# Expert tiles of a routed layer: plain f32 products against three products of high and low parts

## The chip, the core and the metric

One core of one Trainium2 chip runs the whole program. The metric is the device time of one launch in microseconds (us). Three runs of the kernel before gave 783.53, 786.41 and 776.94 us.

## The reference

2048 tokens of 256 numbers (`x`) pass four blocks, each added to `x` after a layer norm:

```
x = x + attn_a(norm(x))     # gated recurrence along the tokens, 6 heads of 64
x = x + ffn(norm(x))        # 8 experts, the best 2 per token
x = x + attn_b(norm(x))     # windowed attention, 16 heads of 16
x = x + ffn(norm(x))        # the same experts again

def ffn(h):
    probs = softmax(h @ router.T);  vals, idx = top_k(probs, 2);  vals /= vals.sum()
    for gup, dp, weight in experts:                  # gup 352x256, dp 256x176
        gate, up = split(h @ gup.T, 2)
        out += weight[:, None] * ((silu(gate) * up) @ dp.T)
```

All of it is float32.

## The kernel before

**Stages.** The program runs five stages, one after the other: the recurrence (0 to about 218 us of the profile), the expert tiles for the first time (222 to 334), the attention (lead-in 334 to 363, periods to 645), the expert tiles again (645 to 757), and the last adds and stores. Each stage's instructions stand in a `Block` (the one of `experts` is L1242); at its end all engines meet at a barrier, so the engine with the longest list holds the others.

**Routing.** Each token's row, with its weights and its number, is sent to the DRAM tensor `xs` by `pool_scatter` (L1181), an indirect DMA that GpSimd (POOL) issues: 8 per group of 512 tokens. Three of the four groups are sent before the expert stage. The last one is routed inside it: `pe_logits`, then compare and choose on VectorE (DVE), `pe_ranks`, and the 8 sends, which POOL issues in turn with its other work at tiles 3 to 10 (`SEND_AT`). The 39 tiles of 128 rows come in two parts (`PART`): tiles 0 to 16 need only the first three groups, tiles 17 to 38 need every row sent.

**One expert tile** (`experts`, L1188). SyncE (SP) loads 128 rows into `xin`, a ring of four (`load`, L1244 to L1257); before tile j+4 is loaded, tile j must have been turned and `aim` (L1417 to L1432, three small DVE operations that read `xin`) must be done. PE turns the rows (`x_transposed`, L1318), ACT copies them out (`x_out`, L1384), PE makes gate and up (`gate_up`, L1334, two products of 128x128 by 352 columns), ACT applies silu (L1391), DVE multiplies (`hidden`, L1439), PE turns the result (L1344), DVE copies it out (`hidden_out`, L1446), PE makes the second product (`down`, L1356, two of 88x128 by 256 columns), ACT scales it (`y_copy`, L1399) and POOL sends it to `back` (`send_back`, L1292). All operands are plain f32, and each such product stands in the trace as two records. PE's order in step s is gate_up(s), hid_transposed(s-1), x_transposed(s+1), down(s-2). SP also loads the attention's small weights in step 12 (`LEAD_FROM`).

**Products of split operands.** The recurrence and the attention use another way: an operand is split into a high part (ACT copies it into an F32R tensor) and a low part (DVE subtracts the high part), and a product is made as high by high, high by low and low by high, all F32R (L351, L362, L1701, L2229).

**Around the attention.** POOL fills the padding rows of `QS` and `KS` with 12 memsets (`pad`, L1829). They are issued within the first expert stage, between its sends. In the lead-in (`lead_*`, L1945 to L2000) SP brings the experts' results back, the four engines add and normalize pairs of blocks, and SP stacks the first keys and queries. The periods follow (`PERIODS`, 20 of them with 5 steps each; the program order of each engine is written out by step). Both expert weights of the second time are loaded by SP in period 15.

Of the kernel before, what the change touches and what calls it, by code (L numbers as in the profile page):

```python
# [62 lines left out]
def build(nc, t, out):  # L63

    ctx = ExitStack()
    with ctx:
# [14 lines left out]
        xTh = sb("xTh", [P, KD, PAD + T], F32R)  # L81
        xTl = sb("xTl", [P, KD, PAD + T], F32R)
# [92 lines left out]
        m = Routed(nc, ctx, t, sem, xTf)  # L175
# [8 lines left out]
        m.down.close()  # L184
        lead, periods = attention(nc, t, m, *common, ident)
# [11 lines left out]
def recurrence(nc, t, x, xn, xTh, xTl, xTf, yT, psY, bank, t0, tl, credit, tail_stats_dve, tail_xn_dve, tail_split_dve,  # L197
# [4 lines left out]
    with ctx:  # L202
# [33 lines left out]
        rms = sb("rms", [P, TPC * HA])  # L236

# [73 lines left out]
        with nc.Block() as block:  # L311
# [195 lines left out]
            def _(act):  # L507
# [49 lines left out]
                tail_act(act, t0, 0)  # L557
                def angle_weights(u):
                    act.wait_ge(folded, 7 + u)
                    act.activation(wfh[:, :, :, u * P:(u + 1) * P], kq[:, :, :, u * P:(u + 1) * P], ACT.Copy).then_inc(wfh_done, 1)  # L560
# [15 lines left out]
                for it in range(NCH):  # L576
                    squares(it)
                    means(it)
                    if it + 1 < NCH:
                        rounded(it + 1)  # L580
                    if it == 0:
                        tail_act(act, t0, 3)
                    else:
                        if it == 2:
                            act.wait_ge(m.filled, 16 * FILLS)
                        tail_rows_act(act, tl, it - 1)
                    if it + 1 < NCH:
# [12 lines left out]
            def _(pool):  # L600
# [34 lines left out]
                for it in range(NCH):  # L635
# [5 lines left out]
                    if it + 1 < NCH:  # L641
                        decays(it + 1)
                    if it > 1:
# [12 lines left out]
            def _(dve):  # L656
# [151 lines left out]
                for it in range(NCH):  # L808
# [27 lines left out]
                    if it > 0:  # L836
# [3 lines left out]
                        group.payload(xn)  # L840
                    if ahead:
# [9 lines left out]
                table.rows()  # L851


class Routed:


    def __init__(self, nc, octx, t, sem, xTf):
# [42 lines left out]
        self.sent, self.d_in = sem("f_sent"), sem("f_d_in")  # L900

    def open_down(self, nc, turn):
        self.wd = self.down.enter_context(nc.sbuf_tensor(f"f_wd{turn}", [FK, 2, NE * 2 * FH], F32, side="right"))

# [13 lines left out]

    def load_up(self, sp):
        for k in range(KD):  # L920
            sp.dma_start(self.gu[:, k], self.wgu_in_dram[k * P:(k + 1) * P]).then_inc(self.w_in, 16)
# [31 lines left out]
YB = 4  # L953
# [234 lines left out]
def experts(nc, m, x, xn, xTh, xTl, xTf, stats, meanvar, vareps, rstd, minus_half, bank, osem, sems, ident, last, lead=None,  # L1188
# [4 lines left out]
    XB = 4  # L1193
    SEND_AT = 3
    LEAD_FROM = 12
# [10 lines left out]
    with ctx:  # L1206
        def sb(name, shape, dt=F32):
            return ctx.enter_context(nc.sbuf_tensor(f"f{turn + 1}_{name}", shape, dt))

        xin = sb("xin", [P, XB, XW])  # L1210
        xt = sb("xt", [P, 2, D])
        act_g = sb("act_g", [P, 2, FH])
        hid = sb("hid", [P, 2, FH])
        hT = sb("hT", [FK, 2, 2 * P])
        yout = sb("yout", [P, YB, D])
        second = sb("second", [P, AR])
        share = sb("share", [P, AR])
        target = sb("target", [P, AR], U32)
        back = sb("back", [P, NGRP, 2, TPC, D]) if last else None

        psG, psH, psY = bank[0], bank[1], bank[2]
        psX, psZ = bank[3][:, 0], bank[3][:, 1]

        x_in = [sem(f"x_in{i}") for i in range(XB)]
        tx_done, xt_done = sem("tx"), sem("xt")
# [1285 lines left out]
```

## Time and profile before

| | |
|---|---|
| median of 3 runs | 783.53 us |
| lowest and highest | 776.94, 786.41 us |
| profiled execution, first to last instruction (its span) | 780.9 us |
| mean granted TensorE clock | 0.848 |
| busy: PE, DVE, POOL, ACT | 83%, 60%, 44%, 38% |

The profile gives no other time of its own execution than its span; the median is 2.6 us above it. In a row of the timeline stand the start, the time from the first start to the last end of the merged instructions, engine, line, operation, what is written from what, and in brackets how long the engine was idle before and for whom it waited. PE is the matmul side of TensorE. Matmuls are pipelined, so what counts is the distance between starts.

### The profile page before, as it was taken

The page shows a single profiled execution, that of the slowest core. Times are in us where ns is not written, and L with a number is a line of the kernel's source. Part 1 is how long each engine was busy: PE and PEld are TensorE (multiplying, and loading weights), DVE is VectorE, ACT ScalarE, POOL GpSimd, SP SyncE. Part 2 cuts the span into 40 slices and gives each one's busy share as a digit, 9 for nine tenths or more (in the row PEclk, how much of TensorE's full clock was granted, in tenths as well). Part 3 has the DMA queues.
Part 4 walks back from the last instruction along what each step waited for, and adds up shares of the span by engine and source line. Part 5 has one row for each costly group of instructions (what it writes and reads, how often), then busy time and mean ns, then how long its engine had stood idle before and what let it go on. Part 6 is the DMA issues. An engine that isn't in the chain of part 4 may idle for free. (4 is left out here: it accounts for less than half of the span.)

```text
span 780.9 us, 14537 instructions
## 1 busy us (share of the span) xinstructions
PE 645.8 (83%) x4707; PEld 503.9 (65%) x4707; DVE 466.2 (60%) x1226; ACT 296.7 (38%) x567; POOL 342.0 (44%) x406
## 2 busy tenths in 40 slices
PE   0889999994569999924689999999899868999960
PEld 0668787773447677713578788878778645777740
DVE  6894859787626434463665767876852454644423
ACT  1363444351014444432344545545433322444430
POOL 4304051616413767743513434445545470653335
PEclk9989999895858999956669999999965555999995
DMA  8699400151122633275432340431307211443329
GB/s 268 214 351 350 149 1 8 37 116 44 43 65 85 195 104 97 85 233 88 81 56 30 83 81 12 76 89 50 80 16 201 100 58 44 134 140 97 102 74 315
DMA packets 68317, 86.92 MB, mean 111 GB/s; under 512 B 8909, under 2 KB 62802, under 8 KB 67380
## 3 DMA queue, kind: packets, MB, share of 16 engines
q1 hardware_dynamic: 61428, 67.80, 32.4%
q0 software_dynamic: 6816, 18.19, 6.5%
q8 instruction: 41, 0.67, 0.4%
q14 instruction: 32, 0.26, 0.1%
HBM read 35.13 MB, written 39.06 MB: 95 GB/s over the span
## 5 line engine op out<-in xcount | busy, mean ns | idle before, releaser
L1292 POOL DMA_INDIRECT back<-f_yout,f_target x78 | 76.7, 983 | 113.7 <-ACT f_yout L1399 103.0
L1334 PE MATMUL bank<-f_wgu,f_xt 128*128 x312 | 113.7, 489 | 3.4 <-ACT f_xt L1384 3.3
L1181 POOL DMA_INDIRECT xs<-xn,f_slots x64 | 65.0, 1016 | 56.7 <-ACT xn L1172 41.1
L1439 DVE TENSOR_TENSOR f_hid<-f_act_g,bank 128x176 f32<-128x176 f32 x78 | 26.3, 338 | 104.5 <-ACT f_act_g L1391 100.4
L2066 POOL TENSOR_SCALAR_AFFINE_SELECT b_prob<-b_prob 128x512 f32<-128x512 f32 x60 | 38.1, 635 | 112.7 <-ACT b_prob L2307 112.4
L2307 ACT ACTIVATE b_prob<-bank 128x1024 f32<-128x1024 f32 x60 | 61.4, 1023 | 55.8 <-PE bank L2146 55.5
L1356 PE MATMUL bank<-f_wd,f_hT 88*128 x312 | 81.4, 385 | 0.0
L1334 PEld LDWEIGHTS bank<-f_wgu,f_xt 128*128 128x128 f32 x312 | 59.1, 199 | 31.3 <-issue 9.9
L2376 DVE COPY_PREDICATED bank<-b_later,bank 128x512 f32<-128x512 int32 x60 | 41.6, 694 | 47.0 <-PE bank L2116 42.4
L1356 PEld LDWEIGHTS bank<-f_wd,f_hT 88*128 88x128 f32 x312 | 54.2, 193 | 4.8
L1399 ACT ACTIVATE f_yout<-bank,f_share 128x256 f32<-128x256 f32 x78 | 36.9, 473 | 39.9 <-PE bank L1356 38.9
L1391 ACT ACTIVATE f_act_g<-bank 128x176 f32<-128x176 f32 x78 | 24.7, 317 | 67.0 <-PE bank L1334 67.0
L2380 DVE TENSOR_REDUCE b_m<-bank 128x4 f32<-128x512 f32 x64 | 44.2, 691 | 8.1 <-PE bank L2107 6.0
L2187 PE MATMUL bank<-b_prob,b_V 128*17 128x128 f32 x992 | 45.6, 307 | 2.1 <-POOL b_prob L2068 2.0
L2146 PE MATMUL bank<-b_QS,b_KS 64*128 64x128 f32 x496 | 45.7, 298 | 0.8 <-ACT b_prob L2307 0.6
L2068 POOL TENSOR_SCALAR_AFFINE_SELECT b_prob<-b_prob 128x512 f32<-128x512 f32 x64 | 40.9, 638 | 11.4 <-ACT b_prob L2304 11.4
L2146 PEld LDWEIGHTS bank<-b_QS,b_KS 64*128 64x128 f32 x496 | 40.8, 215 | 3.4 <-ACT b_prob L2307 2.2
L1384 ACT ACTIVATE f_xt<-bank 128x256 f32<-128x256 f32 x78 | 29.9, 383 | 26.0 <-PE bank L1318 17.7
L2116 PE MATMUL bank<-b_KS,b_QS 48*128 48x256 f32 x208 | 32.6, 362 | 7.8 <-DVE b_m L2380 7.7
L351 PE MATMUL bank<-xTh,wfh 128*128 128x512 f32 x64 | 30.2, 472 | 8.4 <-DVE wfl L705 8.4
L1344 PEld LDWEIGHTS bank<-ident_sb,f_hid 128*88 128x88 f32 x156 | 19.3, 125 | 21.7 <-issue 13.8
L1318 PE MATMUL bank<-ident_sb,f_xin 128*128 128x128 f32 x156 | 32.0, 289 | 1.5 <-DMA f_xin<-xs 1.5
(313 smaller groups left out, 1519.4 us busy)
## 6 DMA issues: line engine op xcount, KB each, us to landing
xs<-xTf SPq DMA_DIRECT2D x8, 2176.0 KB, 19.3
f_xin<-xs SPq DMA_DIRECT2D x78, 136.0 KB, 2.1
f_wgu<-in_wgu SPq DMA_DIRECT2D x4, 1408.0 KB, 14.3
f_wgu<-back SPq DMA_DIRECT2D x16, 256.0 KB, 5.1
b_KS<-b_kh SPq DMA_DIRECT2D x32, 128.0 KB, 3.9
b_QS<-b_qh SPq DMA_DIRECT2D x32, 128.0 KB, 3.9
f_back<-back SPq DMA_DIRECT2D x8, 512.0 KB, 7.5
f_wd<-in_wd SPq DMA_DIRECT2D x4, 968.0 KB
```

The lines of the kernel that those rows point to most:

```text
L1181: pool.indirect_dma_start(m.xs, bass.IndirectOffsetOnAxis(m.slots[:, g, c, i:i + 1], 0), xn[:, g * TPC + i], None)\
L1292: pool.indirect_dma_start(m.back, bass.IndirectOffsetOnAxis(target[:, g % AR:g % AR + 1], 0), yout[:, g % YB], None, bounds_check=2 * 2 * ...
L1334: mm = pe.matmul(psG[:, g % 2, 0:2 * FH], xt[:, g % 2, k * P:(k + 1) * P], m.gu[:, k, bass.ds(e, 2 * FH)], start=k == 0, stop=k == KD - 1)
L1356: mm = pe.matmul(psY[:, g % 2, 0:D], hT[:, g % 2, k * P:(k + 1) * P], m.wd[:, k, bass.ds(e, D)], start=k == 0, stop=k == 1)
L1399: act.activation(yout[:, g % YB], psY[:, g % 2, 0:D], ACT.Copy, scale=share[:, g % AR:g % AR + 1])\
L2066: pool.affine_select(halves_of[:, :, 0], halves_of[:, :, 0], [[0, 4], [-1, P]], ALU.is_gt, 0.0, base=0, channel_multiplier=1)
L2068: pool.affine_select(halves_of[:, :, 1], halves_of[:, :, 1], [[0, 4], [1, P]], ALU.is_ge, 0.0, base=0, channel_multiplier=-1).then_inc(kep ...
L2146: mm = pe.matmul(own_t[:, half, i, w], KS[rows, 2 * u + i, ring(b - 1 + w)], QS[rows, 2 * u + i, ring(b)], start=True, stop=True)
L2187: mm = pe.matmul(psO[CG * j:CG * j + HV1, u * P:(u + 1) * P], V[:, (b - 1 + w) % RING, 4 * u + j], prob[:, quad(b, u) % 2, half, c:c + P], ...
L2307: ins = act.activation(dst, psT[:], ACT.Exp, scale=SCALE)
L2376: dve.copy_predicated(own_s[:, :, :, 1], later[:].unsqueeze(1).unsqueeze(1).broadcast_to([P, 2, 2, P]), own_s[:, :, :, 0]).then_inc(sel_do ...
L2380: dve.tensor_reduce(mo[:, :, 2 * u:2 * u + 2], own_s[:, :, :, 1], AX.X, ALU.max).then_inc(m_done, 1)
```

## The change

- In `experts` both products become three products of F32R operands. Tokens: `x_high` (ACT copy) and `x_low` (DVE subtraction) replace `x_out`; hidden: `hid_high` and `hid_low` replace `hidden_out`.
- Tokens are turned two tiles ahead, into two halves of `bank[3]`; `down` follows three steps behind gate_up (`DOWN_AFTER`). PE's order in step s is gate_up(s), x_transposed(s+2), down(s-3), hid_transposed(s-1).
- The weights are split beforehand: the low part is written over the raw weights, the high part goes to new tensors (`guh`; `wdh`; the first time `wd_high` lies over `xTh`/`xTl`). First time: ACT copies and POOL subtracts quarters of gate/up in turns 1 and 2 of the recurrence; ACT copies and DVE subtracts quarters of down in its last turn, the last two at DVE's end. Second time: eighths of gate/up in periods 15 to 17 and of down in periods 18 and 19, ACT and DVE.
- The tile buffers lie over `QS` and `KS`. So the 12 memsets leave the first expert stage: POOL waits for the last sends, makes 4 before its part of the lead-in and 8 after it.
- The gate/up weights of the second time are loaded in periods 5 and 7, the down weights in period 16.

```diff
 recurrence, act, turn it, behind means(it):
+                    if 0 < it < NCH - 1:
+                        up_high(2 * it - 2)
+                        up_high(2 * it - 1)
+                    if it == NCH - 1:
+                        down_high(0)
+                        down_high(1)
...
 recurrence, pool, behind decays(it + 1):
+                    if 0 < it < NCH - 1:
+                        for q in (2 * it - 2, 2 * it - 1):
+                            pool.wait_ge(m.up_high, q + 1)
+                            m.up_low_part(pool, 0, q)
...
 recurrence, dve, last turn behind payload, and at the end:
                 table.rows()
+                for q in (2, 3):
+                    dve.wait_ge(m.dn_high, q + 1)
+                    m.down_low_part(dve, 0, q)
...
+    def up_low_part(self, eng, turn, q):
+        part = self.eighth(q) if turn else self.quarter(q)
+        eng.tensor_tensor(self.gu[:, :, part].bitcast(F32R), self.gu[:, :, part], self.gu_high[turn][:, :, part].bitcast(F32),
+                          ALU.subtract).then_inc(self.up_low, 1)
...
 experts, gate_up:
-                    pe.wait_ge(xt_done, g + 1)
+                    pe.wait_ge(xtl_done, g + 1)
...
                     for k in range(KD):
-                        mm = pe.matmul(psG[:, g % 2, 0:2 * FH], xt[:, g % 2, k * P:(k + 1) * P], m.gu[:, k, bass.ds(e, 2 * FH)],
-                                       start=k == 0, stop=k == KD - 1)
+                        for xx, w in ((xth, guh), (xth, gul), (xtl, guh)):
+                            mm = pe.matmul(psG[:, g % 2, 0:2 * FH], xx[:, g % 2, k * P:(k + 1) * P], w[:, k, bass.ds(e, 2 * FH)],
+                                           start=n == 0, stop=n == 3 * KD - 1)
+                            n += 1
...
 experts, pe:
                 x_transposed(0)
+                x_transposed(1)
                 for s in range(STEPS):
                     if s < G:
                         gate_up(s)
                     if s == RANKS_AT:
-                        pe_ranks(pe, m, turn, g3, psZ[:, P:2 * P])
+                        pe_ranks(pe, m, turn, g3, ranks)
+                    if s + 2 < G:
+                        x_transposed(s + 2)
+                    if 0 <= s - DOWN_AFTER < G:
+                        down(s - DOWN_AFTER)
                     if 0 <= s - 1 < G:
                         hid_transposed(s - 1)
-                    if s + 1 < G:
-                        x_transposed(s + 1)
-                    if 0 <= s - 2 < G:
-                        down(s - 2)
...
 experts, dve:
+                x_low(0)
+                x_low(1)
                 group.compare()
                 group.choose()
                 for s in range(STEPS):
                     if s < G:
                         hidden(s)
-                    if 0 <= s - 1 < G:
-                        hidden_out(s - 1)
+                    if s + 2 < G:
+                        x_low(s + 2)
                     if s < G:
                         aim(s)
+                    if 0 <= s - 1 < G:
+                        hid_low(s - 1)
...
 experts, pool:
-                    if not last and j >= LEAD_FROM and j % 2 == 0 and (j - LEAD_FROM) // 2 < lead["pads"]:
-                        lead["pad"](pool, (j - LEAD_FROM) // 2)
...
+                    for r in range(YB):
+                        pool.wait_ge(y_out[r], 16 * uses(tile_no(turn, G), r, YB))
                     lead["pool"](pool)
...
         def lead_pool(pool):
-            padded(pool)
+            for i in range(4):
+                pad(pool, i)
+            padded(pool, 1)
...
             pair_deviation(pool, FIRST_PAIRS)
+            pool.wait_ge(u_off, FIRST_PAIRS + 1)
+            for i in range(4, 12):
+                pad(pool, i)
+            padded(pool, RING // 2)
...
 attention:
+        UP_LOADS = {5: 0, 7: 1}
+        UP_PARTS = [(15, 0), (15, 3), (16, 0), (16, 1), (17, 0), (17, 1), (17, 3), (17, 4)]
+        DOWN_PARTS = [(18, 0), (18, 1), (18, 2), (18, 3), (18, 4), (19, 0), (19, 3), (19, 4)]
```

## Rows read from the trace of the kernel before

**Rows 1.** The page: busy time of PE, its granted clock in 40 slices

```profile
PE 645.8 (83%) x4707; PEld 503.9 (65%) x4707; DVE 466.2 (60%) x1226; ACT 296.7 (38%) x567; POOL 342.0 (44%) x406
PEclk9989999895858999956669999999965555999995
```

**Rows 2.** Timeline, one tile of the first expert stage

```profile
301.71 1.35 PE L1334 MATMUL bank<-f_wgu,f_xt 128*128 x4
...
302.90 0.38 PE L1344 MATMUL bank<-ident_sb,f_hid 128*88 128x128 f32 x2
...
303.34 1.03 PE L1356 MATMUL bank<-f_wd,f_hT 88*128 x4
...
304.20 1.35 PE L1334 MATMUL bank<-f_wgu,f_xt 128*128 x4
...
304.41 0.15 DVE L1431 SCALAR_TENSOR_TENSOR f_target<-f_second,f_xin 128x1 uint32<-128x1 f32 x1
```

**Rows 3.** Timeline, F32R products of 256 columns, at full clock and at half

```profile
424.95 0.28 PE L2229 MATMUL bank<-b_boh,b_oTl 128*128 128x256 f32 x1
...
425.07 0.28 PE L2229 MATMUL bank<-b_bol,b_oTh 128*128 128x256 f32 x1
...
640.19 0.41 PE L2229 MATMUL bank<-b_bol,b_oTh 128*128 128x256 f32 x1
...
640.41 0.41 PE L2229 MATMUL bank<-b_boh,b_oTh 128*128 128x256 f32 x1
```

**Rows 4.** One line, L1257 (the loads of a tile's rows): from issue to landing

```profile
DMA to landing us min/median/max: 2.0/2.1/4.0
```

**Rows 5.** Timeline, second expert stage: POOL's sends, the load of tile 17, the last copy

```profile
650.31 0.95 PE L1334 MATMUL bank<-f_wgu,f_xt 128*128 x1 [0.56 <-ACT f_xt L1384]
...
672.08 0.97 POOL L1292 DMA_INDIRECT back<-f_yout,f_target  x1 [1.52 <-DVE f_tiles L1133]
673.36 0.96 POOL L1181 DMA_INDIRECT xs<-xn,f_slots  x1 [0.30 <-DVE f_second L1426]
...
691.32 0.97 POOL L1181 DMA_INDIRECT xs<-xn,f_slots  x1 [0.30 <-ACT f_yout L1399]
...
696.91 0.38 PE L1318 MATMUL bank<-ident_sb,f_xin 128*128 128x128 f32 x2
...
755.00 0.47 ACT L1399 ACTIVATE f_yout<-bank,f_share 128x256 f32<-128x256 f32 x1 [0.39 <-PE bank L1356]
```

**Rows 6.** Timeline, recurrence: subtractions and copies on GpSimd and VectorE

```profile
14.93 3.38 POOL L609 TENSOR_TENSOR f_wgu<-gate,w 128x512 f32<-128x512 f32 x2
17.22 2.17 DVE L700 TENSOR_TENSOR f_wgu<-f_wgu 128x1024 f32<-128x1024 f32 x1
...
21.65 1.22 DVE L700 TENSOR_TENSOR f_wgu<-f_wgu 128x1024 f32<-128x1024 f32 x1
...
113.74 1.28 POOL L619 TENSOR_TENSOR sgl<-sg,sgh 12x512 fp32r<-12x512 f32 x1 [4.46 <-ACT sgh L523]
...
184.63 1.76 DVE L768 TENSOR_TENSOR gate<-gate,o 128x1536 f32<-128x1536 f32 x1
```

**Rows 7.** Timeline, the end of the recurrence on VectorE and ScalarE

```profile
216.07 0.17 DVE L1160 SCALAR_TENSOR_TENSOR f_done<-f_done,f_tiles 128x8 f32<-128x8 f32 x1
216.99 1.02 ACT L171 ACTIVATE xTf<-bank 128x1024 f32<-128x1024 f32 x1 [12.91 <-PE bank L162]
```

**Rows 8.** One line, L1829 (the memsets); timeline of the lead-in's end

```profile
L1829 POOL MEMSET b_QS<- x6: 1796/1798/1800, 272.0 to 319.1; 32x2048 f32 x6
...
358.24 0.20 POOL L1894 TENSOR_TENSOR b_u_shift<-b_u_rstd,b_u_mv 128x2 f32<-128x2 f32 x1
...
366.92 0.59 PE L2100 MATMUL bank<-b_eye,b_maskT 128*128 128x128 bf16 x4 [10.17 <-DMA b_QS<-b_qh]
```

**Rows 9.** Timeline, the attention's last chain

```profile
637.23 0.24 DVE L2403 RECIPROCAL b_rinv<-bank 128x16 f32<-128x16 f32 x1
...
644.58 0.38 ACT L2337 ACTIVATE xTf<-bank 128x256 f32<-128x256 f32 x1 [4.69 <-PE bank L2247]
```

More of the change, by code:

```diff
@@ L236, in recurrence @@
         rms = sb("rms", [P, TPC * HA])
+        m.gu_high.append(sb("guh", [P, KD, NE * 2 * FH], F32R))
         F = 2 * P
@@ L557, in _, with up_high, down_high @@
                 tail_act(act, t0, 0)
+                def up_high(q):
+                    act.wait_ge(m.w_in, 16 * KD)
+                    act.activation(m.gu_high[0][:, :, m.quarter(q)], m.gu[:, :, m.quarter(q)], ACT.Copy).then_inc(m.up_high, 1)
+                def down_high(q):
+                    act.wait_ge(m.d_in, 32)
+                    act.wait_ge(vg_ready, now(NCH - 1, NVG, NVG))
+                    act.activation(m.wd_high[0][:, :, m.quarter(q)], m.wd[:, :, m.quarter(q)], ACT.Copy).then_inc(m.dn_high, 1)
                 def angle_weights(u):
@@ L840, in _ @@
                         group.payload(xn)
+                    if not ahead:
+                        for q in (0, 1):
+                            dve.wait_ge(m.dn_high, q + 1)
+                            m.down_low_part(dve, 0, q)
                     if ahead:
@@ L1208, in sb @@
             return ctx.enter_context(nc.sbuf_tensor(f"f{turn + 1}_{name}", shape, dt))
[L1210 to L1219, printed above, removed]
+        xin, xth, xtl, act_g, hid, hTh, hTl, yout, second, share, target = m.tile_buffers
+        guh, wdh = m.gu_high[turn], m.wd_high[turn]
+        gul, wdl = m.gu[:].bitcast(F32R), m.wd[:].bitcast(F32R)
+        back = m.both_halves[:, 0:NGRP * 2 * TPC * D].bitcast(F32).rearrange("p (g e b d) -> p g e b d", g=NGRP, e=2, b=TPC)
         psG, psH, psY = bank[0], bank[1], bank[2]
-        psX, psZ = bank[3][:, 0], bank[3][:, 1]
+        psX = bank[3]
+        logits, ranks = psY[:, 0, D:2 * D], psY[:, 1, D:2 * D]
         x_in = [sem(f"x_in{i}") for i in range(XB)]
-        tx_done, xt_done = sem("tx"), sem("xt")
+        tx_done, xth_done, xtl_done = sem("tx"), sem("xth"), sem("xtl")
         gu_done, silu_done, hid_done = sem("gu"), sem("silu"), sem("hid")
-        th_done, hT_done = sem("th"), sem("hT")
+        th_done, hTh_done, hTl_done = sem("th"), sem("hTh"), sem("hTl")
         dn_done, y_done = sem("dn"), sem("y")
@@ L1453, in _ @@
                 group, table = Routing(dve, m, turn, g3), Table(dve, m, turn, 1)
-                group.take(psZ)
+                group.take(logits)
+                x_low(0)
+                x_low(1)
                 group.compare()
@@ L1567, in attention @@
         later = sb("later", [P, P], I32)
+        vbuf = sb("V", [P, RAW])
+        with ExitStack() as tiles_too:
+            routing.take_tile_buffers(nc, tiles_too)
         QS = sb("QS", [P, SLOTS, RING * P], F32R)
```

150 lines of the change are left out of this document (111 added, 39 removed).

## The prediction

> **What bounds the kernel now.** I read the page first: PE is busy for 645.8 of 780.9 us, more than any other engine, and its granted clock falls to half in a few stretches only, most of them in the attention [rows 1]. A busy share is an average, so each stage was then read by its own timeline.
>
> The expert tiles are bound by PE. In the timeline of one tile gate_up starts at 301.71 and the next at 304.20, a period of 2.49 us, and PE's own work fills it: gate_up until the transposes start at 302.90 (1.19), the transposes up to `down` at 303.34 (0.44), `down` until the next gate_up (0.86) [rows 2]. 78 such periods are 194 us. Two things other than PE stand at the edge of this stage. The load of a tile takes 2.0 to 4.0 us, 2.1 as a rule, from issue to landing [rows 4]. And in tiles 3 to 10 POOL issues two indirect DMAs per tile, 1.28 us apart, so 2.56 per tile, a little more than PE's period: the fifteen issues between 672.08 and 691.32 are evenly 19.2/15 = 1.28 [rows 5]. Tile 17 may only be loaded once the last of them has landed, and its transpose runs at 696.91 [rows 5], 46.6 behind the first gate_up at 650.31, in step 16: 16 periods are 39.8, its place in the step is 1.4, and the first tiles with the ranks of the last group take the other 5.4. PE doesn't idle ahead of it, so both limits fall together there.
>
> The recurrence is bound by VectorE with POOL and ScalarE beside it, and ends with VectorE's list at 216.24 and ScalarE's at 218.01 [rows 7]. The lead-in is a chain of small steps that ends in SP's stacking of the first keys; POOL's part is over at 358.44, and PE's first product runs at 366.92, waiting for that DMA [rows 8]. The attention's tail is a chain over VectorE, PE and ScalarE that ends at 644.96 [rows 9].
>
> **Tile period.** Six F32R products replace four records each time. F32R products of 256 columns follow each other in 0.12 us at full clock (0.117 over the whole run of them; taken), in 0.22 at half [rows 3]. For 352 columns nothing in the trace is F32R; bounds are 0.117 x 352/256 = 0.161 and 0.117 + 96/256 x 0.111 = 0.158 (the slope alone without a fixed part), so gate_up is 6 x 0.158 = 0.95, `down` 6 x 0.117 = 0.70, and with the transposes' 0.44 a period is 2.09, against 2.49: 0.40 less. At half clock it is about 6 x 0.30 + 0.88 + 6 x 0.22 = 4.0, an estimate.
> Does something else become the bound? ScalarE gets one small copy more, VectorE one subtraction in place of ScalarE's copy; both stay near 1.5 us per tile, three or four operations of less than 0.5 (0.47 the copy out [rows 5]). The loop of the loads shrinks too: with tokens turned two tiles ahead, the buffer is free when aim(s) has run, 2.7 us behind gate_up(s) (in the trace 304.41 + 0.15 is 2.85 behind 301.71 [rows 2]; gate_up's shorter by 0.24, the subtractions are longer by about 0.1), plus 0.2 to issue and 2.1 to land [rows 4] is 5.05, and x_transposed(s+4) is due at 2 x 2.09 + 0.95 = 5.13. It just fits, with nothing left for a load of 4.0. I take 2.15 per tile; bounds 2.09 and 2.5.
>
> In a sentence apart: the Trainium skill ("FP8 and Floating Point Precision", TensorE Precision Notes) counts four passes for a true FP32 product; three of four would save a quarter of 2.05, 0.51 a tile, and by it the sum would be lower by some 5 us over the tiles that don't wait. The rows' 0.40 is used.
>
> **Where that gain goes.** POOL's two-DMA pace of 2.56 per tile doesn't change, and it starts when tile 3 has been scaled, in step 6 of 2.15 instead of step 5 of 2.49: the same 12.5 to 13 us behind the first gate_up, with the same 5.4 of the first tiles on top. So tile 17 can't be turned before about 697 on the old clock, while PE comes to it in step 15, at 650.3 + 15 x 2.15 + 0.95 + 5.4 = 688.9. PE stands still for some 8 us, and its clock, at full before, will fall for a while behind the wait (as it does after other gaps in the page [rows 1]); I take 2.3 us for that. From 696.91 the old kernel needs 58.1 us to the start of its last copy at 755.00 [rows 5]. The new one needs 1.1 to gate_up(16), 22 x 2.15 = 47.3 to gate_up(38), 5.0 for the drain (silu, product, turn, split and `down`, three steps behind), and the 2.3: 55.7, so -2.4, and -0.3 for the last send. Tokens turned ahead and cheaper products save 2.0 in the first tiles. Second time: **-4.7** (bounds -10 and +1). First time: the same pace of POOL, but there the memsets no longer stand between the sends, which takes 1.2 more: **-6** (-12, +1).
>
> **Recurrence.** POOL subtracts two quarters in each of turns 1 and 2. A quarter is 1408 elements per partition; POOL's row of 512 lasts 1.28 [rows 6], so 3.5 each, 7.0 per turn. They come right behind `decays`, whose 1.28 row is at 113.74 in turn 1, and this is where VectorE's taps and other operations with two SBUF inputs run. What both do at once the trace shows at the start: VectorE's subtraction over 1024 elements took 2.17 beside POOL's and 1.22 alone [rows 6], so 0.95 was lost to one overlap. Lower bound 0: VectorE has other work to overlap with. Upper: 1.5 us waited for each quarter in part of its run, plus POOL's own delay of what VectorE needs next, 5 per turn. I take 4 per turn, **+8**, nearest to the row that shows the loss. In sentences apart: the Trainium skill ("SBUF — State Buffer", SBUF: two separate sides) has the shared port pair of VectorE and GpSimd as an exclusive lock, taken for a whole instruction by whichever starts first, which concerns a VectorE operation with two SBUF inputs. By it, two locks of 3.5 us less the time at which VectorE arrives would cost up to 4.9 per turn, and the sum would be 2 higher; the row at 17.22 agrees in kind.
> ScalarE's quarters, 1.4 each by 1024 elements in 1.02 [rows 7], lie in its idle time while it waits for PE or VectorE (12.91 in one piece at the end [rows 7]); nothing. Without that cover they would cost 2.8 a turn. VectorE's first two quarters of down lie in the last turn's idle time likewise. Its last two, 1.76 x 1408/1536 = 1.6 each [rows 6], stand behind its last operation at 216.24: VectorE ends at 219.5, 1.5 behind ScalarE's 218.0: **+1.5** (0, +3).
>
> **Lead-in.** The twelve memsets of 1.80 [rows 8] lay between sends for free. Four now stand ahead of POOL's first addition (7.2 us, of which about 5.5 pass while the results come back; +1.75), eight behind its last step: 358.44 + 1.75 + 14.4 = 374.6. All engines wait for POOL's list at the barrier, and PE starts at about 375.4 instead of 366.92 [rows 8]: **+8.5** (+4 if the first products still wait for something that now overlaps, +12).
>
> **Attention.** In periods 15 to 17 eighths of 704 elements: ScalarE 0.8, VectorE 0.9 each (scaled as above) on engines that mostly wait for PE there: +1.5 (0, 5). In periods 18 and 19 the eight down parts, 6.4 on ScalarE and 7.2 on VectorE, stand in the lists among normalizing, subtracting and the statistics, the steps of the last chain [rows 9]. VectorE idles there for PE and ScalarE; I count about a half as exposed with their waits: **+6** (2, 9), 7.5 with the ones before.
>
> **Sum.** +8 + 1.5 - 6 + 8.5 + 1.5 + 6 - 4.7 = +14.8 on 780.9, 795.7; the profiled execution stands 2.6 under the median, so **798 us** on the median's basis.
>
> **Rivals.**
> *The splitting is hidden* (other side): VectorE's critical operations in turns 1 and 2 don't meet POOL's, and the eighths fall in idle time. For: both engines are at 60% and 38% [rows 1]. Against: the loss in [rows 6], and the place right behind `decays`. It takes away 8 + 1.5 + 6 (the lead-in's 8.5 stays): 783.5 + 14.8 - 15.5 = 783. It decides from the point where less than 1 us a turn is lost.
> *The tiles give their full gain* (other side, further): PE isn't held at tile 17, for instance because POOL's pace quickens once its waits for the tile's aim are met. Then 78 x 0.40 = 31 replaces 10.7: 798 - 20 = 778. Against: 0.96 to 0.97 of the 1.28 is the issue itself and the 0.30 is in every row [rows 5].
> *The loads set the period*: many land in more than 2.1 us, and the period is 2.35. Then 2 x 23 x 0.2 = 9 more: 807.
> *The clock doesn't hold* in the tile loop after the waits: 20 tiles at 4.0 instead of 2.15 are +37: 835.
>
> **Chances.** The forecast 0.45 (787 to 809); hidden 0.22; full gain 0.13; loads 0.12; clock 0.08. The attention's own stretches of half clock [rows 1] may shift with its start, several us either way, which is in all of them. The three runs of before spread over 776.9 to 786.4, so about 2% can be told from no change: 767.9 and 799.2 are the bounds. Faster by over 2%: 0.11 (most of it the full gain, some of the hidden). Slower: half the forecast, the loads and the clock, 0.40. The rest, 0.49, is the same. Range 772 to 814; it leaves out the clock's case and the ends of the gain's.
>
> **What the changed kernel would show.** gate_up in records 0.158 apart and periods of 2.1 to 2.2 at full clock; fourteen or fifteen POOL issues at 1.28 and an idle PE of about 8 us ahead of tile 17's transpose, in both expert stages; in turns 1 and 2 a VectorE operation with two SBUF inputs of twice its length beside POOL's 3.5 us; eight memsets between POOL's last step of the lead-in and the barrier, PE's first product of the attention 8 us further behind the last copy; a start of the second expert stage at about +12. Wrong would be: tile 17 without a wait, memsets hidden behind the stacking, or a VectorE that is as fast in turns 1 and 2 as before.

## The result, and the profile after

The changed kernel took 803.28 us (median of 5 runs, 799.7 to 820.5) against 782.31 for the kernel before (5 runs, 776.9 to 786.4): a ratio of 1.027, interval 1.020 to 1.034. It is slower; whether by more than 2% is left open, as the interval begins just there. The forecast was 798, with 772 to 814 as its range. The profiled execution of the changed kernel (812.6 us) and one more of its five runs (820.5) were slow ones, with a mean granted clock of 0.828 and 0.819 against 0.838 to 0.841, and the ratio leaves them out. The profile spans 810.9 us, some 9 above what the median would give; where those 9 lie is read below, so that they are not put down to the change.

The page of the changed kernel, busy time and granted clock, beside [rows 1]:

```profile
PE 634.9 (78%) x5019; PEld 533.3 (66%) x5019; DVE 538.4 (66%) x1324; ACT 334.1 (41%) x669; POOL 360.3 (44%) x410
...
PEclk9999999886759899955657999978985665989995
```

PE has 11 us less work than before and the span is 30 longer: the products did get cheaper, and the time went where PE waits. What each tile became is seen in the timeline of one tile of the second expert stage, the counterpart of [rows 2]:

```profile
742.78 0.41 PE L1402 MATMUL bank<-xTboth,f_xth 128*128 x1
743.03 0.32 PE L1402 MATMUL bank<-f_wgu,f_xth 128*128 x1
743.19 0.32 PE L1402 MATMUL bank<-xTboth,f_xtl 128*128 x1
...
743.83 0.38 PE L1384 MATMUL bank<-ident_sb,f_xin 128*128 128x128 f32 x2
743.96 0.36 PE L1428 MATMUL bank<-f_wdh,f_hTh 88*128 x1
...
744.75 0.38 PE L1413 MATMUL bank<-ident_sb,f_hid 128*88 128x128 f32 x2
744.89 0.41 PE L1402 MATMUL bank<-xTboth,f_xth 128*128 x1
```

Gate/up products stand 0.16 apart (743.03 to 743.19), and the next tile begins 2.11 behind this one, against 2.49. That is the tile that was forecast. But it is the best case: from tile 17's copy to tile 38's it took 44.6 us where the kernel before took 49.1, so 0.2 us per tile and not 0.38.

The spans of the stages, taken from the starts of the rows that bound them (the end of the first turn is ScalarE's copy of its turned tokens, L171; then the first gate_up, the last scaled copy, the attention's first product, the second first gate_up, the last scaled copy, the end):

| us | before | changed | changed, again | all four edits |
|---|---|---|---|---|
| to the end of the first turn | 110.1 | 109.7 | 110.9 | 112.2 |
| the rest of the recurrence | 116.5 | 127.7 | 127.8 | 120.8 |
| first expert stage | 107.0 | 103.3 | 103.2 | 89.1 |
| lead-in | 33.3 | 48.4 | 48.4 | 36.5 |
| attention | 283.4 | 292.3 | 294.9 | 284.3 |
| second expert stage | 104.7 | 103.5 | 103.8 | 91.6 |
| last adds and stores | 25.9 | 26.0 | 26.1 | 26.0 |

The first row differs by up to 6 us among all profiles of this study, with nothing in it changed. The attention differs by more: 284 to 300 us over the kernels with whole split weights. Both are chance in part. The other rows repeat within some 2 us where nothing in them was changed (the second expert stage 103.5 to 105.4 in the kernels with its loop as first changed, 102.4 and 104.7 in two with the old one) and are the ones to read. Two more profiles of the kernel before, with other edits, have 119.3 in the second row, so its 116.5 was a lucky one, and against them the change costs 8.4 there and not 11.2. Of the 9 between the changed kernel's profile and its median, 7 to 8 are in the attention, as far as profiles can tell: three others with split weights need 284.3 to 285.1 for it instead of 292.3.

**The recurrence.** VectorE in the second turn, by tile, and GpSimd beside it in the timeline:

```profile
L754 DVE SCALAR_TENSOR_TENSOR vconv<-vraw,convv,vconv x6: 742/743/743, 121.9 to 125.3; 128x512 f32<-128x512 f32 x6
L750 DVE TENSOR_SCALAR vconv<-vraw,convv x3: 476/476/6140, 115.1 to 121.6; 128x512 f32<-128x512 f32 x3
```

```profile
114.59 6.36 POOL L963 TENSOR_TENSOR f_wgu<-f_wgu,guh 128x1408 fp32r<-128x1408 f32 x2
```

The same place in the kernel before:

```profile
115.51 0.49 DVE L725 TENSOR_SCALAR vconv<-vraw,convv 128x512 f32<-128x512 f32 x1 [1.31 <-ACT vraw L529]
...
118.63 4.06 DVE L729 SCALAR_TENSOR_TENSOR vconv<-vraw,convv,vconv 128x512 f32<-128x512 f32 x6
```

One tensor_scalar of 0.49 us became 6.14: it stood at 115.10 and was done 0.3 us behind the end of both of GpSimd's subtractions, 3.2 each. GpSimd lost nothing. VectorE's first scalar_tensor_tensor stands 6.85 us behind the first tensor_scalar (121.95) where it stood 3.12 behind it before (118.63, behind 115.51): 3.7 us late.

**The lead-in.** GpSimd's memsets, its first addition, and what follows the barrier, beside [rows 8]:

```profile
345.45 3.65 POOL L1927 MEMSET b_QS<- 32x2048 f32 x2 [1.64 <-DMA back<-f_yout,f_target]
349.15 3.73 POOL L1927 MEMSET b_KS<- 32x2048 f32 x2
353.02 1.26 POOL L1977 TENSOR_TENSOR x_tok<-x_tok,f_wgu 128x512 f32<-128x512 f32 x1
...
369.71 3.65 POOL L1927 MEMSET b_QS<- 32x2048 f32 x2
...
380.83 3.65 POOL L1927 MEMSET b_KS<- 32x2048 f32 x2
388.97 0.28 POOL L2153 CAST b_KP<-b_KS 48x128 fp32r<-48x128 f32 x1 [4.49 <-POOLq L1307]
389.07 0.58 PE L2207 MATMUL bank<-b_eye,b_maskT 128*128 128x128 bf16 x4 [20.47 <-PEq L1307]
```

GpSimd's part of the normalizing ends at 369.65; eight memsets take it to 384.5, and the barrier itself 4.5 more. PE stood still for 20.5 us.

**Tile 17.** GpSimd's sends in the second stage, the first gate_up and tile 17's transposes, and PE's waits in that stretch (total, times, longest):

```profile
681.40 0.66 PE L1402 MATMUL bank<-xTboth,f_xth 128*128 x1 [0.17 <-DVE f_xtl L1528]
...
701.61 0.97 POOL L1251 DMA_INDIRECT xs<-xn,f_slots  x1 [0.30 <-issue]
...
719.99 0.98 POOL L1251 DMA_INDIRECT xs<-xn,f_slots  x1 [0.30 <-issue]
...
725.44 0.69 PE L1384 MATMUL bank<-ident_sb,f_xin 128*128 128x128 f32 x2 [5.21 <-DMA f_xin<-xs]
```

```profile
PE bank L1384 <- DMA f_xin<-xs: 5.2, 1, 5.2
```

The pace is the old one, 1.28 us per issue over most of the stretch, and PE waited 5.2 us for the first tile that needs all sends, where in this stage there was no such wait before [rows 5]. PE came to it 38.8 us behind the first gate_up and had it at 44.0.

### The profile page after: what moved, and what is told of

The parts are those of the page before. It is cut to its first block and busy times, and to the rows that moved or that the text cites. A ratio compares the mean times of both kernels' runs of the same rounds, so it can differ in the third digit from the quotient of the medians.

```text
span 810.9 us, 15701 instructions
## 1 busy us (share of the span) xinstructions
PE 634.9 (78%) x5019; PEld 533.3 (66%) x5019; DVE 538.4 (66%) x1324; ACT 334.1 (41%) x669; POOL 360.3 (44%) x410
## 5 line engine op out<-in xcount | busy, mean ns | idle before, releaser
L1251 POOL DMA_INDIRECT xs<-xn,f_slots x64 | 68.9, 1077 | 54.3 <-ACT xn L1242 38.7
L353 PE MATMUL bank<-xTboth,wfh 128*128 128x512 f32 x128 | 48.6, 456 | 8.3 <-DVE wfl L730 8.3
L1402 PE MATMUL bank<-f_wgu,f_xth 128*128 x156 | 52.9, 339 | 0.0
L2175 POOL TENSOR_SCALAR_AFFINE_SELECT b_prob<-b_prob 128x512 f32<-128x512 f32 x64 | 41.0, 641 | 11.7 <-ACT b_prob L2411 11.7
L1428 PE MATMUL bank<-f_wd,f_hTh 88*128 x156 | 44.8, 287 | 0.0
L1384 PE MATMUL bank<-ident_sb,f_xin 128*128 128x128 f32 x156 | 33.4, 298 | 14.4 <-DMA f_xin<-xs 14.2
L1528 DVE TENSOR_TENSOR f_xtl<-bank,f_xth 128x256 fp32r<-128x256 f32 x78 | 33.0, 424 | 16.3 <-ACT f_xth L1458 16.0
L1458 ACT ACTIVATE f_xth<-bank 128x256 fp32r<-128x256 f32 x78 | 30.0, 384 | 32.0 <-PE bank L1384 31.2
L1534 DVE TENSOR_TENSOR f_hTl<-bank,f_hTh 88x256 fp32r<-88x256 f32 x78 | 32.7, 419 | 15.7 <-ACT f_hTh L1465 15.3
L353 PEld LDWEIGHTS bank<-xTboth,wfh 128*128 128x128 f32 x128 | 28.8, 225 | 16.6 <-issue 9.8
```

The source lines that it names most:

```text
L353: last = pe.matmul(psV[:, u], wt[:, k, j, u * P:(u + 1) * P], xx[:, k, cols], start=n == 0, stop=n == 3 * KD * TAPS - 1)
L1251: pool.indirect_dma_start(m.xs, bass.IndirectOffsetOnAxis(m.slots[:, g, c, i:i + 1], 0), xn[:, g * TPC + i], None)\
L1384: mm = pe.transpose(psX[:, g % 2, k * P:(k + 1) * P], xin[:, g % XB, k * P:(k + 1) * P], ident[:])
L1402: mm = pe.matmul(psG[:, g % 2, 0:2 * FH], xx[:, g % 2, k * P:(k + 1) * P], w[:, k, bass.ds(e, 2 * FH)], start=n == 0, stop=n == 3 * KD - 1)
L1428: mm = pe.matmul(psY[:, g % 2, 0:D], hh[:, g % 2, k * P:(k + 1) * P], w[:, k, bass.ds(e, D)], start=n == 0, stop=n == 5)
L2175: pool.affine_select(halves_of[:, :, 1], halves_of[:, :, 1], [[0, 4], [1, P]], ALU.is_ge, 0.0, base=0, channel_multiplier=-1).then_inc(kep ...
```

## The experiments

Twelve kernels were run, each but the one of experiment 11 timed several times in turn with the kernel before.

**1. The same subtractions, behind the tensor_scalars.**

```diff
+                            pool.wait_ge(tap_done, now(it + 1, VT, NTAP))
                             m.up_low_part(pool, 0, q)
```

> The same work as the changed kernel, but in turns 1 and 2 GpSimd's two subtractions of 3.2 us wait until VectorE's three tensor_scalar of the first tap (L750) are done, so they meet the scalar_tensor_tensor (two SBUF inputs) instead. Theory A: only the tensor_scalar is held off by GpSimd for as long as its instruction lasts, and the others run beside it: L750 is back at 0.49, L754 stays at 0.74 to 0.8, VectorE's delay of about 5 us a turn is gone, and the first gate_up starts 7 to 9 us earlier than at 237.4; about 795 us in all. Theory B (every VectorE operation with two SBUF inputs is held off too): a scalar_tensor_tensor of 6 us stands where the tensor_scalar stood, the first gate_up moves by less than 2 us, 803 us. Theory C (GpSimd's own lateness is what counts, by what is queued behind the subtractions): no better either, and no VectorE instruction is stretched.

VectorE's taps of the second turn, by tile:

```profile
L755 DVE SCALAR_TENSOR_TENSOR vconv<-vraw,convv,vconv x5: 737/746/3673, 121.2 to 129.7; 128x512 f32<-128x512 f32 x5
L751 DVE TENSOR_SCALAR vconv<-vraw,convv x3: 486/486/489, 118.1 to 120.8; 128x512 f32<-128x512 f32 x3
```

```profile
121.43 7.12 POOL L964 TENSOR_TENSOR f_wgu<-f_wgu,guh 128x1408 fp32r<-128x1408 f32 x2 [3.85 <-DVE vconv L751]
```

Theory B in its core. The tensor_scalars are back at 0.49, and two scalar_tensor_tensors take 3.67 and 3.64 instead of 0.75, one beside each subtraction. Not one of 6 us: here VectorE and GpSimd took turns, and GpSimd's two needed 7.1 instead of 6.4. It even lost more (second turn 49.2 us against 47.4, third 47.8 against 45.6), since the old place had had VectorE's idle time between the tensor_scalars to use (0.84 and 0.91 us in this trace). 816.28 us, ratio 1.040 (1.029 to 1.051). So the delay follows GpSimd's instruction wherever it is put beside VectorE's work.

**2. GpSimd's subtractions left out.**

```diff
-        part = self.eighth(q) if turn else self.quarter(q)
+        part = self.eighth(q) if turn else slice(self.quarter(q).start, self.quarter(q).start + 8)
```

> Leaves out GpSimd's part of the first splitting: of each quarter only 8 columns are subtracted, so the low part of the gate/up weights of the first time is wrong and its time missing; ScalarE's copies and VectorE's down parts stay. Theory A (GpSimd's subtractions cost what the recurrence lost): first gate_up at about 228.5 instead of 237.4, -9; about 794 us. Theory B (ScalarE's copies of 1.4 us and the down parts at the end cost the larger part): first gate_up at 233 or later, less than -4.

The first turn's end to the first gate_up is 120.7 us against 127.7: 7.0 gone, the turns at 43.7 and 41.9 instead of 47.4 and 45.6, so 3.7 each. Theory A, with 7 instead of 9; what is left is 1.4 above the 119.3 of two other profiles without any splitting, the price of VectorE's last two quarters. 796.97 us, ratio 1.020 (1.010 to 1.030).

**3. The memsets spread.** KS's six between the sends of the first stage, QS's on three engines:

```diff
+                    if not last and j >= LEAD_FROM and j % 2 == 0 and (j - LEAD_FROM) // 2 < 6:
+                        lead["pad_k"](pool, (j - LEAD_FROM) // 2)
...
+            act.activation(QS[r:r + 32, :, ring2(hc)], src, ACT.Copy, scale=0.0).then_inc(q_pads, 1)
```

> The six memsets of KS go back between GpSimd's sends of the first expert stage (the tile buffers don't reach KS), of those of QS two go to ScalarE's idle time ahead of its first normalizing, two to GpSimd's end and two to VectorE's end of the lead-in. Theory A (the memsets on GpSimd's list are the whole loss of the lead-in): the attention's first product stands 33 to 35 us behind the last scaled copy instead of 48.4 (33.3 before the change), -14; about 789 us. Theory B (the longer drain, the barrier or SyncE's stacking hold it as well): 40 or more, no better than -8.

The lead-in of this kernel in the timeline:

```profile
346.14 3.84 ACT L1938 ACTIVATE b_QS<-ident_sb 32x2048 fp32r<-32x2048 f32 x2 [2.39 <-DMA back<-f_yout,f_target]
...
368.09 3.65 POOL L1933 MEMSET b_QS<- 32x2048 f32 x2
368.18 1.76 DVE L1933 MEMSET b_QS<- 32x2048 f32 x1 [0.48 <-issue]
...
376.68 0.28 POOL L2164 CAST b_KP<-b_KS 48x128 fp32r<-48x128 f32 x1 [4.94 <-POOLq L1307]
...
376.81 0.59 PE L2218 MATMUL bank<-b_eye,b_maskT 128*128 128x128 bf16 x4 [10.47 <-PEq L1307]
```

35.4 us behind the last copy instead of 48.4, a little over what theory A allowed (33 to 35). Theory A in substance: 13 of the 15 lost us went with the memsets. The edit also takes GpSimd's wait for the last sends off its list and makes ScalarE's copies of the small weights before it waits for them, so the 13 are those of the whole edit. 793.15 us, ratio 1.011 (0.999 to 1.023).

**4. The sends three tiles earlier.**

```diff
-    SEND_AT = 3
+    SEND_AT = 0
```

> The last group's eight sends are issued between the send_backs of tiles 0 to 7 instead of 3 to 10. Theory A (tile 17 waits for GpSimd's last send, three of its steps of 2.56 too late): PE's waits for tile 17 (5.2 us in the second stage, 3.0 in the first) are gone, GpSimd's last send is 6 to 8 us earlier, each stage 4 to 6 us shorter, about 794 us. Theory B (the loop of the loads sets the pace anyway, or the sends wait for the payload): the waits shrink, but the stages stay within 2 us, 801 us.

PE's wait for tile 17 is gone in the second stage and the stage is 97.5 us instead of 103.5; in the first PE still waits 2.65 us for it, and the stage gained only 2.5 (100.8). Theory A for one stage, between A and B for the other. 800.82 us, ratio 1.022 (1.012 to 1.032), not the 794 that was expected: the gain of 8.5 doesn't show in the time. In the profiled execution (814.86 us) the attention took 300.5 us; where the other three (796.5 to 804.0) lost it no trace shows.

**5. The low parts on VectorE.** Two quarters in its last turn of the recurrence, two at the start of the expert stage; GpSimd's lines go:

```diff
+                    if not ahead:
+                        for q in (0, 1):
+                            dve.wait_ge(m.up_high, q + 1)
+                            m.up_low_part(dve, 0, q)
...
+                if not last:
+                    for q in (2, 3):
+                        dve.wait_ge(m.up_high, q + 1)
+                        m.up_low_part(dve, 0, q)
                 group.take(logits)
```

> All four subtractions of the gate/up quarters leave GpSimd for VectorE, 1.65 us each: two where VectorE waits 3.9 us for PE in the recurrence's last turn, two where it waits 3.6 us for the last group's logits at the start of the first expert stage. The result stays the reference's. Theory A (GpSimd's instructions hold VectorE's own for their whole length, so the same work on VectorE in its idle time costs nothing): first gate_up within 1 us of the run that leaves the work out, 230 to 232, 6 to 8 us earlier than with GpSimd; about 796 us. Theory B (VectorE's list is full, 6.6 us more on it are 6.6 us later): first gate_up at 236 to 238, no gain.

VectorE's four subtractions of gate/up, two and two:

```profile
192.01 3.15 DVE L963 TENSOR_TENSOR f_wgu<-f_wgu,guh 128x1408 fp32r<-128x1408 f32 x2
...
223.89 3.16 DVE L963 TENSOR_TENSOR f_wgu<-f_wgu,guh 128x1408 fp32r<-128x1408 f32 x2 [3.25 <-PEq L180]
```

120.7 us from the first turn's end to the first gate_up, to the tenth what it took with the work left out. Theory A by the trace. The first gate_up stands at 229.2. The time shows nothing of it (803.14 us where 796 was expected, ratio 1.032, 1.023 to 1.040); the attention took 291.8 in the profile. An edit of 7 us can't be judged by the total here, and is by its own stretch.

**6. Six load buffers.**

```diff
-XB, YB = 4, 4
+XB, YB = 6, 4
```

> The ring of loaded tiles has six buffers instead of four, nothing else. Theory A (the round of a load, from aim over the issue to the landing, is at the edge of two periods and stretches tiles to a mean of about 2.4 us against PE's 2.11): behind tile 17 the copies follow each other in 2.11 to 2.15 with few exceptions, 22 tiles x 0.25 = 5 to 6 us less in each stage; before it the gain goes into a longer wait for tile 17. About 793 us. Theory B (PE waits for ScalarE and VectorE, the longer intervals stay): mean still 2.35, no gain over 2 us.

PE's waits around tile 17 in its second stage:

```profile
PE bank L1384 <- DMA f_xin<-xs: 7.7, 1, 7.7
```

Theory A in the stages, not in the time (793 was expected). From tile 17 to tile 33 every copy follows the last in 2.11 to 2.14 us (the last five come closer together, as they did before), and tiles 17 to 38 take 40.9 to 41.0 us instead of 44.6. Before tile 17 the faster tiles only lengthened the wait, 5.2 to 7.7. Stages of 96.4 and 97.9. The time was 802.17 us, ratio 1.027 (1.020 to 1.035): no gain over the changed kernel, though its stages are 12.5 us shorter. Its four runs had a mean clock of 0.820 to 0.827, against 0.838 to 0.841 in the changed kernel's three fastest, and the attention of its profile took 292.6. Why all four ran at the lower clock is not shown.

**7. Both.**

> Six buffers, and the sends between the send_backs of tiles 0 to 7. Theory A (two limits in turn, and PE's own 2.11 behind them): the gains add, 10 to 13 us less than the changed kernel in the second stage, 7 to 10 in the first, last copies 90 to 93 us behind the first gate_up in the second stage; about 784 us. Theory B (behind the two lies a third one, GpSimd's own 2.56 us per tile while it sends): the second stage stays at 96 us or more.

Stages of 89.5 and 88.1 us: 13.8 and 15.4 less than the changed kernel, more than the two edits by themselves (9.4 and 11.6), as each had run into the other's limit. Theory A. 782.62 us in ten runs, ratio 0.997 (0.990 to 1.004): level with the kernel before.

**8. The second splitting left out.**

```diff
-                            part = m.eighth(UP_PARTS.index((n, u)))
+                            part = m.first8(UP_PARTS.index((n, u)))
...
-        part = self.eighth(q) if turn else self.quarter(q)
+        part = self.first8(q) if turn else self.quarter(q)
```

> Leaves out most of the second splitting: of each eighth only 8 columns are subtracted on VectorE, and of gate/up only 8 columns are copied on ScalarE (the copies of down stay whole), so the weights of the second expert stage are wrong; all waits stay. Theory A (these parts lie in idle time, which the traces of two undisturbed runs suggest with 284 to 285 us from the attention's first product to the second stage's first gate_up, against 283.4 before the change): no more than 2 us less; about 801 us. Theory B (as predicted, 7.5 us exposed, and the granted clock hides it): that stretch is 277 to 279 us, 796 us.

276.9 us from the attention's first product to the second stage, which is theory B's number, and the time is 794.04, ratio 1.018 (1.008 to 1.027). But the stretch doesn't speak for B as it stands: half clock took 79 us of it, 100 or 101 in the profiles that needed 284 to 285 with the splitting in place. The run is inconclusive on the clock, and the price has to be read from pieces with the same clock.

The splitting stands behind the reciprocal of the twelfth of the 16 blocks; up to there the two kinds of kernel run alike wherever the clock is the same. The last two reciprocals and the second stage's first gate_up, in the kernel before and in the changed one (for the first [rows 9] and [rows 5] have the other two rows):

```profile
625.53 0.26 DVE L2403 RECIPROCAL b_rinv<-bank 128x16 f32<-128x16 f32 x1 [2.70 <-PE bank L2199]
```

```profile
651.88 0.24 DVE L2521 RECIPROCAL b_rinv<-bank 128x16 f32<-128x16 f32 x1
...
665.06 0.24 DVE L2521 RECIPROCAL b_rinv<-bank 128x16 f32<-128x16 f32 x1
```

The tail behind the last reciprocal is 13.1 us before (12.9 in two more profiles with plain tiles) and 16.3 to 16.4 with the splitting, and the block ahead of it 11.7 (12.1 and 12.1) and 13.2 to 13.5: 3.4 and some 1.3 us, where the last two gate/up parts and the eight down parts stand. With most of the parts out they are 14.9 and 12.2. Between the twelfth and the fifteenth reciprocal stand six of the eight gate/up parts, and the stretch takes the same time without and with them at the same clock, in experiments 10 and 11:

```profile
573.02:628.09 55.07, 51.83 (x430) 40.81 (x428) 22.84 (x56) 18.85 (x34) 26.38 (x39) 0.55 0.38 113
```

```profile
600.14:655.34 55.20, 51.93 (x430) 40.91 (x430) 28.45 (x61) 22.90 (x40) 26.94 (x39) 0.55 0.22 60
```

So the splitting costs nearly 5 us, all of it at the end. (The windows show start and end, length, busy time of PE, its weight loads, VectorE, ScalarE and GpSimd, PE's granted clock, and the transfers.)

**9. All four edits (3, 5, 6 and the sends).**

> The changed kernel with all four edits: gate/up's low parts on VectorE in its idle time, the memsets spread, six load buffers, the sends between tiles 0 to 7. The result stays the reference's. Theory A (the change was held back by four costs of its own and each edit takes its own one away, so they add): first gate_up at 229 to 231, first stage 89 to 91 us, lead-in 35 to 36, attention 284 to 287, second stage 88 to 89; span 752 to 757, time about 756 us, 3.5% less than before the change. Theory B (what is gained comes back as lower granted clock, or one limit replaces another): above 770 us.

760.56 us in six runs, ratio 0.974 (0.967 to 0.980): 21 us less than the kernel before and 43 less than the change as it was made. The stages are in the table above. Theory A; the 4 us beyond what was expected are the first turn (112.2) and a second stage of 91.6, in which PE still waited 2.4 us at tile 17.

**10. The kernel before with its sends earlier** (`SEND_AT = 0`, nothing else).

> The kernel before the change with the last group's sends between the send_backs of tiles 0 to 7, nothing else. Theory A (its tiles are bound by PE at 2.49, so earlier sends only take away what little PE waited at tile 17): 2 to 3 us less in the first stage, 0 to 1 in the second, no difference that can be measured. Theory B (the late sends held the kernel before as well): 5 us or more less in a stage, 773 us.

782.77 us in ten runs, ratio 1.003 (0.999 to 1.007). Its stages took 106.2 and 100.5 us. Theory A in time; of the stages, the first gave 0.8 us where 2 to 3 were expected, the second 4.2 where 0 to 1 were, with 9 us less of half clock in it. So what frees the split tiles is worth little to the plain ones, which PE bounds.

**11. The changed kernel again.**

> The changed kernel once more, for a second profile. Theory A (what the first profile of it shows over the other runs, a stretch of half clock some 150 us into the attention, worth 6 us, comes and goes by itself): 284 to 293 us from the attention's first product to the second stage's first gate_up, every other stretch within 1 us of the first profile. Theory B (it belongs to the change): the stretch is there again, 292 us.

One run, 816.86 us. Every stretch but the attention is within 1.2 us of the first profile, the attention 294.9, with the stretch of half clock at the same place: theory B.

**12. The kernel before with the memsets late.**

> The kernel before the change, with plain f32 tiles and unsplit weights, in which only the twelve memsets stand as in the changed one: GpSimd waits for the last sends, makes four ahead of its part of the lead-in and eight behind it. Theory A (the move of the memsets alone costs what the lead-in lost): the attention's first product 47 to 49 us behind the last scaled copy instead of 33.3, 13 to 15 us slower, about 795 us; the second expert stage is as before. Theory B (part of the loss comes from the tile buffers that lie over QS and KS, and from the longer drain): 42 us or less. Beside it, of the clock: if the longer idle of PE in the lead-in brings the stretch of half clock about 150 us into the attention, it is here too and the attention takes 290 to 294 us; if it comes with the split products or the split weights, the attention takes 282 to 285 us as before.

```profile
377.87 3.65 POOL L1829 MEMSET b_KS<- 32x2048 f32 x2
...
386.11 0.58 PE L2106 MATMUL bank<-b_eye,b_maskT 128*128 128x128 bf16 x4 [21.10 <-PEq L1242]
```

The lead-in takes 47.0 us: theory A, 13.7 us for an edit with no split product in it. 797.13 us, ratio 1.011 (1.002 to 1.020). And the stretch of half clock came along. By windows of one same piece of the attention, between the reciprocals of the eighth and the ninth block, in the kernel before:

```profile
513.80:527.90 14.10, 13.64 (x177) 11.51 (x175) 9.46 (x20) 7.44 (x14) 6.83 (x12) 1.00 0.54 124
```

in the changed one:

```profile
537.50:557.40 19.90, 19.61 (x178) 16.19 (x175) 9.56 (x21) 7.67 (x14) 6.92 (x12) 0.66 0.38 89
```

in the kernel before with late memsets:

```profile
534.50:554.40 19.90, 19.62 (x179) 16.19 (x175) 9.55 (x21) 7.66 (x14) 6.89 (x12) 0.66 0.40 88
```

and in the one with all four edits:

```profile
505.60:519.80 14.20, 13.73 (x177) 11.61 (x175) 9.55 (x21) 7.44 (x14) 6.91 (x12) 1.00 0.52 124
```

The same instructions, 5.8 us longer at 0.66. Of the ten profiles with a lead-in of 46.9 us or more, eight have it; of the four with 33 to 37, none. It doesn't take split products, since the kernel before with late memsets has it too. But that kernel's attention took 284.7 us as a whole, not the 290 to 294 that were expected of one with this stretch: the half clock behind it was shorter, 104 us in all against 109 in the kernel before. So 5.8 is what the stretch costs where it stands, and not what it adds to the attention.

## Why the prediction was right, and where it was not

The direction, the size (14.8 over the profile forecast, 21 between the medians) and each of the four places of loss were right; the range held. Term by term, against the stretches of the table:

- *Tile period.* 2.09 to 2.15 forecast, 2.11 measured, from pitches of 0.16 and 0.12. Of the two prices that were weighed the rows' 0.40 was the better: 0.38 a tile, not 0.51.
- *The load loop.* "It just fits" was the step that failed in the stages. It left 0.08 us for a load of 2.1, so at the edge every delay of aim or of a landing goes into PE's list. The rival *the loads set the period*, given 0.12, was half true: 44.6 us for tiles 17 to 38 instead of 40.9, 3.7 us per stage (experiment 6). So the second stage gained 1.2 instead of 4.7, the first 3.7 instead of 6.
- *Tile 17.* Right in kind and place: GpSimd's pace held PE in both stages. Of the 8 us of waiting 5.2 came (3.0 in the first stage): PE was there 38.8 us behind the first gate_up, as forecast (38.6), but the tile at 44.0 and not at 46.6, since GpSimd's last send stands 38.6 behind the first gate_up and no longer 41.0. The forecast had booked most of that apart, as 2.0 saved in the first tiles. With six buffers PE comes earlier and waits 7.7, and from tile 17's transposes to the last copy it then takes 55.7 us, the forecast's number; with four it takes 59.5. Experiment 4 takes the second stage's wait away. The clock fell at the wait as assumed, to half for 6.8 us in each stage.
- *Recurrence.* +8 forecast, 7.0 measured by leaving the work out, and +1.5 against 1.4 for the end. The kind of loss was right, the instruction that it fell on was another. The text looked for operations with two SBUF inputs; the one that paid was a tensor_scalar with one, held for two instructions of GpSimd. The Trainium skill's page "SBUF — State Buffer" (SBUF: two separate sides) covers both, an operation in a two-port mode and one with two SBUF inputs; the traces agree that both kinds are held, with 6.14 against 0.49 for the tensor_scalar and 3.67 against 0.75 for the other, but no trace shows in which mode the tensor_scalar ran.
- *Lead-in.* +8.5 forecast, +15.1 measured: the largest mis-sized term. The eight memsets were counted right (14.4 us, 14.8 measured), and two things beside them wrong. The four early ones cost 4.1 and not 1.75: GpSimd waits for the last send to land (345.45, 4.75 behind the last copy), its memsets end at 352.88, and its first addition stands 2.5 us further behind the last copy than before (12.3 us at 353.02, and 9.8 in this row of before, with the last copy at 333.62):

```profile
343.41 1.26 POOL L1878 TENSOR_TENSOR x_tok<-x_tok,f_wgu 128x512 f32<-128x512 f32 x1 [7.02 <-DMA f_wgu<-back]
```

The other 1.6 are lost further on, in waiting for VectorE's statistics. And the forecast let PE in 0.8 us behind GpSimd's end, where the barrier takes 4.5. The trace of before has that number too, in a row that the forecast passed over, GpSimd's first instruction behind the barrier, with its idle time in brackets:

```profile
363.27 0.28 POOL L2046 CAST b_KP<-b_KS 48x128 fp32r<-48x128 f32 x1 [4.84 <-POOLq L1242]
```

- *Attention.* +7.5 forecast as exposed splitting, nearly 5 measured: next to nothing for six of the eight gate/up parts (1.5 was forecast for all), 4.7 for the other two and the down parts (6 for down). It came out at +9 in the profile of the changed kernel all the same, with 118 us of half clock where the profiles of 284 to 285 have 100 or 101; the forecast said only that such stretches may shift. That the profile's number is near the forecast's is luck.

The sum forecast 14.8; the profile of the changed kernel says 30, its median 21. The terms as measured, with what the clock added to single profiles left out, are 8.4 for the recurrence, -3.7 for the first expert stage, +15.1 for the lead-in, +4.7 for the attention and -1.2 for the second expert stage: about 23. Too little for the lead-in (6.6) and too much taken off for the stages (5.8) were partly made good by too much for the recurrence and the attention (3.9), which is luck too. "Within 2%" had 0.49 and "slower" 0.40; it was 2.7% slower, with an interval that begins at 2.0. Had the barrier's 3.7 and the four memsets' 2.4 been in the sum, it would have come to 804.

The rival *the tiles give their full gain* is worth a second look. It was the right reading of what the change could do, for another reason than given: GpSimd's pace didn't quicken, but the sends could start earlier, and two more buffers take the loads off the edge. Then the stages are 88 to 92 us, 13 to 18 less than before, and with the other two edits the change pays.

## What to carry to other kernels

Before PE's work in a loop is cut by a sixth, write down the next limits of that loop one by one (here the load's round against the number of buffers, and the sender's pace against the tile that waits for it) and move them in the same change; each alone gave 8.5 and 12.5 us in the stages, both together 29. Work that leaves a hidden place, like twelve memsets, has to be priced where it lands, on the list that ends last before the barrier, with the barrier's own time behind it. Long elementwise work on GpSimd can hold VectorE's next instruction until it is done: 6.4 us of it cost a turn 3.7, what VectorE had no idle time to cover; the same work, 1.6 us a quarter on VectorE itself, was free in its idle time.

## What the runs showed of the hardware that I had not expected

- VectorE's tensor_scalar stayed blocked through two GpSimd instructions in a row (6.14 us), its scalar_tensor_tensor only through one at a time (3.67 and 3.64), and in that case GpSimd's were longer by a tenth (3.55 and 3.6 instead of 3.2).
- A stretch of half clock (13.7 us) stands some 150 us into the attention in eight of ten profiles with a long lead-in (in one of them there are two, from 135 us on), and in none of four with a short one, after 75 to 100 us at full clock. What links it to the lead-in stays open: fourteen profiles show that they mostly go together, and no run was made that changes the lead-in's length alone in small steps.
- With nothing changed in it, the first turn of the recurrence ended between 106.7 and 112.9 us in fourteen profiles.
